# A recommendation tower on one core: products with x once per group of four tiles, as four 32-row tiles

## What is computed

```
e = stack([tbl_f[ids[:, f]] for f in range(39)], axis=1)       # (1024, 39, 16)
x0 = xk = e
outs = []
for W in (f0, f1, f2):                                         # f0 (39*39, 128); f1, f2 (128*39, 128)
    z = einsum('bfd,bgd->bfgd', x0, xk).reshape(b, f * g, d)
    cur = einsum('bpd,pm->bmd', z, W)
    outs.append(cur); xk = cur
z = concatenate(outs, axis=1).sum(-1)                          # (1024, 384)
h = relu(concatenate([z, dense_ctx], 1) @ W_top1 + b_top1)
h = relu(h @ W_top2 + b_top2)
y = h @ W_top3
```

## Time and profile before

| what | us |
|---|---|
| median of three runs (1387.10 to 1389.87) | 1388.26 |
| the profiled execution | 1386.06 |
| its span, from the first to the last instruction | 1383.9 |
| PE busy in it | 1308.5 |
| DVE busy | 1126.5 |
| ACT busy | 905.7 |
| POOL busy | 705.0 |

### The profile page before, as it was taken

One profiled execution on the slowest core, in us unless ns is written; L12 is line 12 of the kernel. 1 busy time (PEld: TensorE's weight loads), 2 busy tenths in 40 slices (PEclk: granted clock), 3 DMA queues, 4 the chain that ended last, 5 costly groups with the idle time before them and its releaser, 6 DMA issues.

```text
span 1383.9 us, 20103 instructions
## 1 busy us (share of the span) xinstructions
PE 1308.5 (95%) x5912; PEld 997.4 (72%) x5912; DVE 1126.5 (81%) x2794; ACT 905.7 (65%) x3233; POOL 705.0 (51%) x698
## 2 busy tenths in 40 slices
PE   1399999999999999999999999999999999999998
PEld 0356776777777777777777777777777777777787
DVE  2068988888888888888888888888888888888885
ACT  2046776766767676677767667676766777676664
POOL 7786556654545556454566545455564532333200
PEclk9989999999999999999999999999999999999999
DMA  5171021100311012110211003110121102110000
GB/s 138 27 224 47 17 71 50 50 27 3 95 30 43 27 38 68 49 30 14 70 50 50 27 4 95 30 43 28 37 69 50 30 12 68 47 47 26 1 2 0
DMA packets 51172, 63.51 MB, mean 46 GB/s; under 512 B 13067, under 2 KB 24344, under 8 KB 51019
## 3 DMA queue, kind: packets, MB, share of 16 engines
q1 hardware_dynamic: 34544, 56.08, 13.1%
q0 software_dynamic: 10128, 2.98, 2.0%
q10 hardware_dynamic: 6392, 3.18, 0.9%
HBM read 11.08 MB, written 1.02 MB: 9 GB/s over the span
## 4 chain that ended last, share of the span: by engine, by line
PE 77%; DVE 10%; ACT 6%; POOL 3%; issue 3%; DMA 1%; ACTq 0%; DVEq 0%
PE Y L763 17%; PE Y L765 16%; PE Y L764 16%; PE C L711 14%; PE C L725 5%; ACT Y L486 5%; PE S L719 4%; POOL rows L347 3%; DVE sum_a L635 2%; DVE sum_a L630 2%; DVE sum_b L630 2%; DVE z L599 1%; PE C L743 1%; PE S L685 1%; DVE cur L655 1%
## 5 line engine op out<-in xcount | busy, mean ns | idle before, releaser
L486 ACT ACTIVATE Y<-Y,x_col 128x128 f32<-128x128 f32 x2944 | 799.1, 356 | 392.6 <-PE Y L765 379.0
L763 PE MATMUL Y<-f_high,cur_high 128*128 128x512 f32 (+1 forms) x1280 | 626.1, 489 | 10.3 <-DVE part L643 5.0
L764 PE MATMUL Y<-f_low,cur_high 128*128 128x512 f32 (+1 forms) x1280 | 496.2, 388 | 0.0
L765 PE MATMUL Y<-f_high,cur_low 128*128 128x512 f32 (+1 forms) x1280 | 495.9, 387 | 0.0
L385 POOL TENSOR_TENSOR pairs<-shifted,base 117x512 f32<-117x512 f32 x186 | 240.0, 1292 | 462.2 <-PE C L711 460.2
L347 POOL DMA_INDIRECT rows<-in_tbl_dram,ids_sb x312 | 306.8, 983 | 76.8 <-issue 62.9
L763 PEld LDWEIGHTS Y<-f_high,cur_high 128*128 128x128 f32 x1280 | 241.6, 189 | 121.9 <-issue 45.1
L764 PEld LDWEIGHTS Y<-f_low,cur_high 128*128 128x128 f32 x1280 | 242.4, 189 | 89.8 <-issue 52.2
L765 PEld LDWEIGHTS Y<-f_high,cur_low 128*128 128x128 f32 x1280 | 240.9, 188 | 48.6
L630 DVE SCALAR_TENSOR_TENSOR sum_b<-Y,x_col,sum_b 128x128 f32<-128x128 f32 x768 | 262.5, 342 | 0.0
L711 PE MATMUL C<-pairs,f_sum 117*128 117x512 f32 (+1 forms) x448 | 231.5, 599 | 5.2 <-DVE pairs L593 5.2
(11 more groups left out here) (83 smaller groups left out, 660.1 us busy)
## 6 DMA issues: line engine op xcount, KB each, us to landing
shifted<-x_seq SPq DMA_DIRECT2D x157, 234.0 KB
base<-x_seq SPq DMA_DIRECT2D x95, 78.0 KB
rows<-in_tbl_dram,ids_sb POOLq DMA_INDIRECT x312
shifted<-x_seq SPq DMA_DIRECT2D x31, 156.0 KB
G<-in_L_rec_f_dram ACTq DMA_DIRECT2D x3, 832.0 KB, 11.8
w_sb<-in_W_top_dram SPq DMA_DIRECT2D x1, 768.0 KB
f_ext<-in_L_rec_f_dram SPq DMA_DIRECT2D x1, 760.5 KB
w_sb<-in_W_top_dram SPq DMA_DIRECT2D x1, 512.0 KB
```

The costliest lines, as they stand in the source:

```text
L486: ins = act.activation(where[:, i * M:(i + 1) * M], where[:, i * M:(i + 1) * M], ACT.Copy, scale=x_col[:, t // JT % QG, t % JT, f:f + 1])
L763: pe.matmul(where, ch, wh, start=True, stop=False)
L764: pe.matmul(where, ch, wl, start=False, stop=False)
L765: pe.matmul(where, cl, wh, start=False, stop=True).then_inc(y_filled, 1)
```

## The change

The product with x is now done once per group for its four tiles, as `g_products(n)`. Each tile's product is cut into four: 32 partitions (2 rows times 16 dimensions) of `cur1` against 80 columns of x (2 rows times 40), each of the four on its own 32 rows of PE's array and into its own bank: S, C and the two banks of a pair of Y. That pair is taken in turn with the units, ahead of unit 1 of the second tile of the next group (`G_UNIT`). The last group does three of its tiles ahead of the last unit (`LAST_G_UNIT`), and the last tile at the end. ACT reads the four banks one after another. The sums of the first cross layer move by one place. POOL spreads x over 2 rows instead of 8, in two operations instead of four. `cur1` gets 8 buffers instead of 2. The diff, cut to its core:

```
-AT_SUM = [12 + 3 * k for k in range(K0)]
-AT_G = 5
-AT_X = 2
+AT_SUM = [13 + 3 * k for k in range(K0)]
+AT_X = 5
+RT = 4
+RB = TB // RT
+G_UNIT, LAST_G_UNIT = (1, 1), (3, 4)
+AT_G = CH + 2 * G_UNIT[1]
+AT_LAST_G = CH * LAST_G_UNIT[0] + 2 * LAST_G_UNIT[1]
+CUR1_RING = 2 * JT
...
+def pair_uses():
+    uses = []
+    for g in range(NG):
+        for j in range(JT):
+            for u in range(UNITS):
+                if g and (j, u) == G_UNIT:
+                    uses.append(("G", g - 1))
+                if g == NG - 1 and (j, u) == LAST_G_UNIT:
+                    uses.append(("G", NG - 1))
+                uses.append(("unit", JT * g + j, u))
+    return uses
...
+PAIR = {u: n % UB for n, u in enumerate(PAIR_USES)}
+PAIR_PREVIOUS = {u: PAIR_USES[n - UB] for n, u in enumerate(PAIR_USES) if n >= UB}
...
                 if g >= 2:
-                    pool.wait_ge(s_filled, S_USE["G", JT * (g - 1) - 1] + 1)
-                for j in range(JT):
-                    ins = pool.tensor_tensor(
-                        x_block[:, q % 2, j, :].rearrange("p (b f) -> p b f", b=TB),
-                        x_col[:, q, j, :].unsqueeze(1).broadcast_to([P, TB, FC]),
-                        block[:].unsqueeze(2).broadcast_to([P, TB, FC]), ALU.mult)
+                    pool.wait_ge(s_filled, S_USE["G", g - 2] + 1)
+                for i in range(RB):
+                    ins = pool.tensor_scalar(x_block[:, q % 2, :, i * FC:(i + 1) * FC], x_col[:, q, :, :],
+                                             half_block[:, i:i + 1], None, ALU.mult)
...
+            def read_g_banks(n):
+                act.wait_ge(s_filled, S_USE["G", n] + 1)
+                read_g(n, 1).then_inc(c_read, 1)
+                read_g(n, 0).then_inc(s_read, 1)
+                read_g(n, 2).then_inc(g_read, 1)
+                read_g(n, 3).then_inc(g_read, 1)
...
-            def g_product(t):
-                s_free(("G", t))
-                pe.wait_ge(acc_steps, NST * (t + 1))
-                if t % JT == 0:
-                    pe.wait_ge(block_made, t // JT + 1)
-                pe.matmul(S[:, 0:TB * FC], cur1[:, t % 2, :], x_block[:, t // JT % 2, t % JT, :],
-                          start=True, stop=True).then_inc(s_filled, 1)
+            def g_products(n):
+                s_free(("G", n))
+                pe.wait_ge(c_read, C_USE["G", n])
+                if n < NG:
+                    _, t, u = PAIR_PREVIOUS["G", n]
+                    pe.wait_ge(acc_steps, NST * t + max(FREED[2 * u], FREED[2 * u + 1]))
+                tiles = g_tiles(n)
+                pe.wait_ge(acc_steps, NST * (tiles[-1] + 1))
+                pe.wait_ge(block_made, tiles[0] // JT + 1)
+                for i, t in enumerate(tiles):
+                    for r in (1, 2, 3, 0):
+                        b = slice(r * RB * D, (r + 1) * RB * D)
+                        ins = pe.matmul(g_bank(n, r)[:, i * RB * FC:(i + 1) * RB * FC], cur1[b, t % CUR1_RING, :],
+                                        x_block[b, t // JT % 2, t % JT, :], start=True, stop=True)
+                ins.then_inc(s_filled, 1)
...
             def chunk(t, c):
-                v = UNITS * t + c // 2 - UB
-                if v >= 0 and (c % 2 == 0 or v % UNITS not in SCALED_UNITS):
-                    pe.wait_ge(acc_steps, NST * (v // UNITS) + FREED[2 * (v % UNITS) + c % 2])
+                previous = PAIR_PREVIOUS.get(("unit", t, c // 2))
+                if previous and previous[0] == "G":
+                    if c % 2 == 0:
+                        pe.wait_ge(g_read, 2 * (previous[1] + 1))
+                elif previous:
+                    _, t0, u = previous
+                    if c % 2 == 0 or u not in SCALED_UNITS:
+                        pe.wait_ge(acc_steps, NST * t0 + FREED[2 * u + c % 2])
```

More of the change, by code:

```diff
@@ L68, with g_tiles @@
 WARM_FIELDS, WARM_PRODUCTS = 5, 28
+def g_tiles(n):
+    if n < NG - 1:
+        return range(JT * n, JT * (n + 1))
+    return range(NT - JT, NT - 1) if n == NG - 1 else range(NT - 1, NT)
 def small_bank_uses():
@@ L94, in sum_bank_uses @@
         m = mlp_in_group(g)
-        if m is not None:
-            uses += [("mlp", m, i) for i in range(3)]
+        stages = [("mlp", m, i) for i in range(3)] if m is not None else []
+        if q == 0:
+            uses += stages
+        if g:
+            uses.append(("G", g - 1))
+        if q:
+            uses += stages
         if g + 1 < NG:
             uses.append(("sum", g + 1))
-    uses.append(("l2", BT - 1, 0))
+    uses += [("G", NG - 1), ("G", NG), ("l2", BT - 1, 0)]
     return {u: n for n, u in enumerate(uses)}
+def pair_uses():
[4 more added lines that the diff above has]
+                if g and (j, u) == G_UNIT:
+                    uses.append(("G", g - 1))
+                if g == NG - 1 and (j, u) == LAST_G_UNIT:
+                    uses.append(("G", NG - 1))
+                uses.append(("unit", JT * g + j, u))
+    return uses
 def mlp_in_group(g):
@@ L247, in load_f0, with pair_bank, g_bank @@
                     eng.dma_start(dst, src).then_inc(f0_in, 16)
+        def pair_bank(pair, i):
+            return Y[:, 512 * (2 * pair + i):512 * (2 * pair + i + 1)]
         def bank(t, c):
-            b = 2 * ((UNITS * t + c // 2) % UB) + c % 2
-            return Y[:, 512 * b:512 * (b + 1)]
+            return pair_bank(PAIR["unit", t, c // 2], c % 2)
         def unit(t, u):
-            b = 2 * ((UNITS * t + u) % UB)
-            return Y[:, 512 * b:512 * (b + 2)].rearrange("p (s m) -> p m s", m=M)
+            pair = PAIR["unit", t, u]
+            return Y[:, 1024 * pair:1024 * (pair + 1)].rearrange("p (s m) -> p m s", m=M)
+        def g_bank(n, r):
+            if r < 2:
+                return (S, C)[r][:]
+            return pair_bank(PAIR["G", n] if n < NG else PAIR["unit", NT - 1, UNITS - 1], r - 2)
         def x_cols(bt, q):
@@ L261, in g_half, with tail_bank @@
             return G[:, (bt % 2) * (FC * P):(bt % 2 + 1) * (FC * P)].rearrange("p (f b) -> p f b", b=P)
+        def tail_bank(m):
+            pair = PAIR["G", NG - 1] if m < 2 else PAIR["unit", NT - 1, 3]
+            return pair_bank(pair, m % 2)[:, 0:P]
         by_dim = rows[:].rearrange("p (f d) -> p d f", d=D)
@@ L473, in split_cur0, with read_g @@
                 act.activation(cur0_high[:, g % 2, :], C[:], ACT.Copy).then_inc(cur0_high_ready, 1)
[L475 to L480, removed]
+            def read_g(n, r):
+                tiles = g_tiles(n)
+                b0, nj = TB * (tiles[0] % TPB), len(tiles)
+                to = g_half(tiles[0] // TPB)[:, :, b0:b0 + TB * nj].rearrange("p f (j r i) -> p r j i f", r=RT, i=RB)
+                return act.activation(to[:, r, :, :, :],
+                                      g_bank(n, r)[:, 0:nj * RB * FC].rearrange("p (j i f) -> p j i f", i=RB, f=FC),
+                                      ACT.Copy)
+            def read_g_banks(n):
[4 more added lines that the diff above has]
+                read_g(n, 3).then_inc(g_read, 1)
             def scale_chunk(t, c):
@@ L654, in tile @@
                 dve.wait_ge(acc_steps, n0 + MERGE)
-                dve.tensor_reduce(cur1[:, t % 2, :], unit(t, 4), AX.X, ALU.add).then_inc(acc_steps, 1)
+                if j == 0 and g >= 2:
+                    dve.wait_ge(s_filled, S_USE["G", g - 2] + 1)
+                dve.tensor_reduce(cur1[:, t % CUR1_RING, :], unit(t, 4), AX.X, ALU.add).then_inc(acc_steps, 1)
             split_cur0(0)
@@ L826, in tail1 @@
             def tail1(m, w, z, start, stop):
-                return pe.matmul(Y[:, (2 + m) * 512:(2 + m) * 512 + P], w[:, m * P:(m + 1) * P], z,
-                                 start=start, stop=stop)
-            pe.wait_ge(acc_steps, NST * t + R1)
+                return pe.matmul(tail_bank(m), w[:, m * P:(m + 1) * P], z, start=start, stop=stop)
+            pe.wait_ge(g_read, 2 * NG)
             for m in range(2):
```

68 lines of the change are left out of this document (44 added, 24 removed).

## The result

| | before | after |
|---|---|---|
| median of the runs, us | 1388.42 (1387.10 to 1389.87) | 1431.82 (1431.03 to 1432.44) |
| span of the profiled execution, us | 1383.9 | 1429.3 |
| mean granted clock in it | 0.996 | 0.987 |

The ratio is 1.0313, with a 95% interval of 1.0301 to 1.0326: 43.4 us slower. The forecast of 1432 us was met to the microsecond. Its terms were not: the largest, the products' 23.9 us, measured little more than a third of that, and two causes that stood in no term, falls of the clock and the place of an array, took up the difference. The sum came out by luck.

A forecast was written before the change was run, and what follows sets the result against it. The prediction took PE as the bound, with DVE close behind. Terms of 19.2 + 23.9 + 1 made +44 us on 1386.06, so 1430; the median, 2.2 us above that execution, gave 1432 us, range 1398 to 1494.

The forecast's parts named there:

- the products' 23.9 us: Sixteen small products in a group's second tile: 2.03 us, 0.77 beyond the free wait, +23.9 us over 31 groups.
- The ring: Second tile: products take a bank pair, so chunk 2 starts 2.24 us late, less 1.62 saved: 0.62 per group, +19.2 us.
- 1.4 with the products in it: Sign of being right: distance from one group's first chunk to the next group's grows by 0.62 + 0.77 = 1.4 us.
- all side by side: Rival, chance 0.24: the four row parts fully overlap, products take 1.15 us, hidden in the wait: 1408 us, or 1391.
- The 78.4 us: Rival, chance 0.26: the products' weight loads go one after another, 3.79 us per group, 2.53 too many: 1488 us.
- ACT's reads at no cost: Reads of the products' four banks: about 454 ns each, at most 1.8 us against 3.6 available, so no cost.
- a rival of 5%: Rival, chance 0.05: load and matmul don't overlap on 32 rows, or PE's clock falls among products: above 1495 us.
- or the clock row falls under 1: Sign of being wrong: the profile's row of PE's granted clock drops below 1; no size given.
- the ends: Group 0 -1.1 us, last group's twelve products 1.6 us, tail about +0.5 us: together +1 us.
- POOL's saving: POOL's spread, 4 x 725 ns a group, becomes at most 1.45 us; priced at nothing, covered by POOL's waits for PE.

The follow-up runs named there:

- the hole: The kernel before, with one pair of banks per group skipped and left unused where the change puts its products; 1.0270 of the kernel before.

## Why the prediction was right, and where it was not

**The ring** was right in mechanism: PE waits some 1.3 us for step 20 in 30 of 31 groups, the hole costs 1.30 us per group when it stands alone, and no chunk waits for ACT's reads. The term was 0.62 us per group. Between groups of like work with the clock up, the difference is 40.56 - 39.38 = 1.18, and 1.13 in the group shown, but 0.59 in the groups that open a batch; over all it is 1.02 (1115.0 - 1087.5 over 27 groups), where I had forecast 1.4 with the products in it. Taking off 0.15 for the place and 0.30 for the products leaves 0.57. That is a remainder and not the ring alone: ACT's longer reads and the late start of the first product, worth 0.2 us each where they were mended alone, are in it. Tile by tile the forecast was further off. With the products' 0.77 us in it, the second tile was to grow by 2.24 - 0.54 + 0.77 = 2.47 us and grew by 2.07. The third and fourth were to give 1.08 together and gave 0.75. The first, whose product I had counted at nothing, gave 0.19. So a product counted in part in each tile, where I had counted it in full or not at all; no run shows which waits had hidden the rest.

**The products themselves** were the step that failed. I took one pass of each product after another, 2.03 us, 0.77 too many, +23.9 us. I said that the first load of the next product can be under way, and then counted as if the two passes of a product kept all others waiting. In fact four chains run beside each other, 32 starts in 0.87 us: the rival "all side by side" had that right. Of the 1.26 us of room they use 0.36 (late start) + 0.87 + 0.20 (way out) = 1.43, and what they cost is the 0.12 us by which chunk 2 is late and the read behind them: 0.3 us per group, 9 us, by the run that leaves out twelve of sixteen. The rule of the Trainium skill in TensorE: Matmul & The Clock Gate, section LDWEIGHTS, that 32 rows load as long as 128, holds nearly for one load (0.186 us against 0.198 to 0.202). The 78.4 us that the prediction worked out for loads that don't overlap did not come: they overlap.

**ACT's reads at no cost** was wrong. I priced them by their number of elements; the new order of writing made each 0.3 us longer, and a sum stands behind the first of them: 5 us in the stretch, mended alone.

**Two causes were in no term.** The clock: nine falls of 1.6 us, 14 us. I named it only in a rival of 5% and as a sign of error ("or the clock row falls under 1"), and by that sign the forecast was wrong while its number was right. The place in SBUF: 4.6 us, by the traces.

The sum as measured, for the 44.5 us by which the time from the first to the last chunk grew: clock 14, products 9, place 5, and 16 left for the ring with ACT's reads. Forecast: 0, 24, 0 and 19, and 1 for the ends, which measured 0.9 (102.8 us outside that stretch before, 103.7 after). That POOL's saving is worth nothing was right: nobody waits for its spread.

**Open.** What exactly makes the clock fall. A hole of the same length before chunks of full width left it up; before sixteen products on 32 rows it fell 4 to 8 times, before four of them 12 times, with products on one row part at a time 21 times, and on all rows 4 times, for 6.8 us each. Matmuls that fill the wait took the falls away. So after waits of 1.0 to 1.5 us a fall came only with small products behind the wait, and after 1.63 and 2.41 us it also came, once each, without them. No run here parts the two further, or says why one group falls and its like does not.

## What to carry to other kernels

Before a unit is put into a full ring of buffers, find the step that frees its place and what PE did in the meantime: the hole cost 1.3 us a group, more than half of the 2.16 us that the old products had taken. Where small products are packed by rows, issue neighbours on different rows, and price what reads them by the order in which it writes. Compare parts, not sums: a total that fits to the microsecond hid a term mis-sized and three costs left out, and a look at the clock by group and at the distance of like instructions found two of these.

## What was not expected of the hardware

- Matmuls on 32 rows start 0.01 us apart across four row parts; the same 32 pairs took 1.07 us up to the next chunk in that order, 2.55 with one row part at a time, and 3.57 on all rows. The next row part did not wait for the end of the one before it: it started when five of its eight pairs had.
- The granted clock fell to half after waits of only 1.3 us with small products behind them, and four unneeded matmuls per group made the kernel 1.1% faster (1.0313 to 1.0201 of before).
- An array of 8 bytes, ahead of the chunks' weights in SBUF, moved the distance of matmuls from 0.230 to 0.232 or 0.234 us, 4.3 us over the stretch by the traces.
- ACT's copy of 320 elements takes 0.45 us with two or eight neighbours written in a row, and 0.77 with each at 512 bytes from the last.
